# Four modulated residual blocks on one core: the first V and `conv0` in fp32, the first pair of samples blurred alone

## The reference

```
def _layer(x, style, w, b, mw, mb, typ):
    s = style @ mw.T + mb
    weight = SCALE * w * s[:, None, :, None]
    demod = lax.rsqrt(jnp.sum(weight * weight, axis=(2, 3)) + EPS)
    weight = weight * demod[:, :, None, None]
    # 'same': conv_same(x, weight) + b
    # 'upsample': conv_transpose by 2 + b, then blur with 2 * [1, 3, 3, 1] / 8
    # 'downsample': blur with [1, 3, 3, 1] / 8, then conv with stride 2, + b
...
for i, typ in enumerate(('same', 'upsample', 'same', 'downsample')):
    out = _layer(out, style, weights[i], biases[i], mod_w[i], mod_b[i], typ)
...
x = x + block(x)      # four times, each with its own weights
```

## Time and profile before

| | |
|---|---|
| median of 3 runs | 1302.7 us (1302.08 to 1303.91) |
| profiled execution, device time | 1303.89 us |
| its span (first to last instruction) | 1302.0 us |
| mean granted TensorE clock | 0.998 of 2.4 GHz |
| busy: PE, DVE, ACT, POOL | 99%, 85%, 71%, 28% |
| instructions | 20375 |

### The profile page before, as it was taken

One profiled execution on the slowest core, in us unless ns is written; L12 is line 12 of the kernel. 1 busy time (PEld: TensorE's weight loads), 2 busy tenths in 40 slices (PEclk: granted clock), 3 DMA queues, 4 the chain that ended last, 5 costly groups with the idle time before them and its releaser, 6 DMA issues.

```text
span 1302.0 us, 20375 instructions
## 1 busy us (share of the span) xinstructions
PE 1291.3 (99%) x6553; PEld 1076.5 (83%) x6553; DVE 1101.5 (85%) x1795; ACT 922.4 (71%) x1773; POOL 359.1 (28%) x640
## 2 busy tenths in 40 slices
PE   8999999999999999999999999999999999999998
PEld 6888888888888888888888888888888888888887
DVE  7999888998898889878889798988878878888885
ACT  6767576676675766766767667667677787787784
POOL 5142311141313212115222222122422252322311
PEclk9999999999999999999999999999999999999999
DMA  9354465545564455655446554556554276565543
GB/s 327 103 168 119 144 179 165 164 116 164 174 174 144 123 155 166 182 151 168 130 152 177 153 164 121 154 172 174 161 158 128 77 159 188 163 189 156 165 126 96
DMA packets 95369, 203.39 MB, mean 156 GB/s; under 512 B 10720, under 2 KB 12256, under 8 KB 95264
## 3 DMA queue, kind: packets, MB, share of 16 engines
q1 hardware_dynamic: 95040, 201.91, 54.0%
q10 hardware_dynamic: 224, 0.18, 0.0%
HBM read 72.39 MB, written 67.24 MB: 107 GB/s over the span
## 4 chain that ended last, share of the span: by engine, by line
PE 98%; DVE 1%; ACT 0%; issue 0%; POOL 0%; POOLq 0%; DVEq 0%; ACTq 0%
PE ps L462 96%; PE ps L586 1%; PE ps L398 1%; DVE scr L945 0%; ACT gh L815 0%; ACT vf L771 0%; PE ps L420 0%; DVE scr L955 0%; DVE scr L954 0%; DVE xl L1036 0%; DVE w2l L1245 0%; DVE w3q L1163 0%; ACT xh L733 0%; POOL scr L1416 0%; POOL scr L1415 0%
## 5 line engine op out<-in xcount | busy, mean ns | idle before, releaser
L462 PE MATMUL ps<-zh,gh 128*128 128x512 f32 (+1 forms) x1028 | 407.0, 396 | 0.2 <-ACT gh L815 0.2
L462 PE MATMUL ps<-zl,gh 128*128 128x512 f32 (+1 forms) x1028 | 405.5, 394 | 0.0
L747 ACT ACTIVATE zh<-ps,t_bx 128x512 fp32r<-128x512 f32 x256 | 175.3, 685 | 285.4 <-PE ps L462 284.4
L462 PE MATMUL ps<-zh,gl 128*128 128x512 f32 (+1 forms) x1028 | 282.2, 395 | 0.0
L787 ACT ACTIVATE kp<-ps,t_T1s 64x256 f32<-64x256 f32 x508 | 210.6, 463 | 66.3 <-PE ps L462 61.4
L1051 DVE SCALAR_TENSOR_TENSOR X<-ps,t_D,X 128x512 f32<-128x512 f32 x255 | 190.1, 745 | 61.1 <-PE ps L462 34.6
L462 PEld LDWEIGHTS ps<-zh,gh 128*128 128x128 f32 x1028 | 193.9, 189 | 46.9 <-DVE zl L1042 1.3
L462 PEld LDWEIGHTS ps<-zl,gh 128*128 128x128 f32 x1028 | 194.1, 189 | 45.0
L462 PEld LDWEIGHTS ps<-zh,gl 128*128 128x128 f32 x1028 | 194.0, 189 | 45.1
L1042 DVE SCALAR_TENSOR_TENSOR zl<-ps,t_bx,zh 128x512 fp32r<-128x512 f32 x256 | 190.7, 745 | 42.9 <-ACT zh L747 40.2
L1377 POOL TENSOR_TENSOR w3h<-w3q,w3h 64x256 fp32r<-64x256 f32 x63 | 69.1, 1097 | 548.5 <-ACT w3h L761 535.0
(11 more groups left out here) (226 smaller groups left out, 1494.5 us busy)
## 6 DMA issues: line engine op xcount, KB each, us to landing
out_x<-X SPq DMA_DIRECT2D x255, 256.5 KB, 5.2
X<-out_x SPq DMA_DIRECT2D x96, 513.0 KB, 7.1
gh<-gh SPq DMA_DIRECT2D x127, 240.0 KB, 3.0
gl<-gl SPq DMA_DIRECT2D x127, 240.0 KB, 3.7
X<-x_in SPq DMA_DIRECT2D x32, 513.0 KB, 7.2
pk<-taps_in SPq DMA_DIRECT2D x3, 512.0 KB, 12.3
pk<-pack_in SPq DMA_DIRECT2D x3, 352.0 KB, 12.5
pk<-sets_in SPq DMA_DIRECT2D x4, 256.0 KB, 8.4
```

The costliest lines, as they stand in the source:

```text
L462: return pe.matmul(out_ap, a, b, start=first, stop=last, skip_group_check=True)
L747: act.activation(zh[n % 2][:, ZPAD:ZPAD + M], ps[:, ZP + n % 2, :], IDENT, bias=tab["bx"][:, k, b:b + 1]).then_inc(s["zhi"], 1)
```

## The change

- V of quad 0 is four fp32 products of the unsplit `w2f` and `w3q` instead of nine fp32r ones; its splits (`w3h`, `w3l` of quad 0) are gone.
- `conv0` of samples 0, 1 and 2 (`WHOLE = 3`) is two fp32 products each, of `X` itself and a copy of the weights scaled by `S0` (`w0s`, made on ScalarE in place of `xhi`); their `xhi` and `xlo` are gone. `conv0(1)` comes before V of quad 1, `conv0(2)` right behind `convg(0)`.
- 14 idle products become 4 products of `w2h`; 6 earlier ones become 5.
- Quad 0 is evicted pair by pair: VectorE and ScalarE first evict samples 0 and 2 (they share one half of the columns of `kp`), whose blur runs at once (`fir0`), then samples 1 and 3; ScalarE takes two of VectorE's four evictions.
- VectorE's `w2l` comes first, `w2dl` and part of `w2d` move from GpSimd to VectorE. ScalarE's `ghi_first(0)` moves ahead of `vfull(1)`, `xhi(2)`, `w3hi(2)`; `w0hi` behind `w3hi(1)`.
- GpSimd waits for `w3qa` before it goes on; the tap sums come before `w1l` and `w1d`; the w3 product of quad 1 waits for V; `w3lo(1)` waits for `bx0`; the w3 product of quad 2 and `w0l` wait for `zlo` 1.

```diff
 def conv0(n):
...
+    if n < WHOLE:
+        p, use = pair_of(n)
+        pe.wait_ge(s_in[p], 16 * use)
+        xn = X[:, where(n)[3], :]
+        for d in range(2):
+            m = add(o, w0s[:, n % 2, 2 * d:2 * d + 2, :], xn[:, d:d + M], first=(d == 0), last=(d == 1))
+        m.then_inc(s["conv0"], 1)
+        return
...
 def v_products(q):
...
+    if q == 0:
+        pe.wait_ge(s["w2f"], 16)
+        pe.wait_ge(s["w3qa"], 1)
+        add(a[:, 0], w2f[:, 0, left, :], w3q[:, 0], first=True)
+        add(a[:, 1], w2f[:, 0, right, :], w3q[:, 0])
+        pe.wait_ge(s["w3q"], 1)
+        add(a[:, 1], w2f[0:C, 0, left, :], w3q[0:C, 1], last=True)
+        add(b, w2f[0:C, 0, right, :], w3q[0:C, 1], first=True, last=True).then_inc(s["V"], 1)
+        return
...
 conv0(0)
-conv0_high(1)
-idle_products(4)
+conv0(1)
 v_products(1)
-idle_products(14)
+for _ in range(4):
+    add(ps[:, OP + 1, 0:256], w2h[:, 0, 0:2, :], w2h[:, 0, :, :], first=True, last=True)
 pe.wait_ge(s["z0"], 1)
 for n in range(NN):
...
     if n == 0:
-        conv0_low(1)
         convg(0)
+        conv0(2)
         k_products(1)
-    elif n + 1 < NN:
+    elif 2 <= n and n + 1 < NN:
         conv0(n + 1)
...
 # ScalarE
 def xhi(n):
...
+    if n < WHOLE:
+        act.wait_ge(s["w0f"], 16)
+        if n >= 2:
+            act.wait_ge(s["conv0"], n - 1)
+        act.activation(w0s[:, n % 2], w0f[:, 0], ACT.Copy, scale=tab["S0"][:, 0, b:b + 1]).then_inc(s["xhi"], 1)
+        return
...
 act.wait_ge(s["t1s"], 1)
-for j in range(QS):
-    ins = evict(0, j, 0)
-ins.then_inc(s["kev"], 1)
+evict(0, 0, 0)
+evict(0, 2, 0).then_inc(s["kev0"], 1)
+evict(0, 1, 0)
+evict(0, 3, 0)
+act.wait_ge(s["kevd"], 1)
+evict(0, 1, 1)
+evict(0, 3, 1).then_inc(s["kev"], 1)
 zhi(0)
+act.wait_ge(s["z0"], 1)
+ghi_first(0)
+xhi(2)
+glo_copy(0)
 vfull(1)
...
 # VectorE
 dve.wait_ge(s["c_small"], 16)
+dve.wait_ge(s["w2hi"], 1)
+dve.wait_ge(s["w2f"], 16)
+dve.tensor_tensor(w2l[:, 0], w2f[:, 0], w2h[:, 0].bitcast(F32), ALU.subtract).then_inc(s["w2l"], 1)
...
-xlo(0)
 dve.wait_ge(s["t1s"], 1)
 dve.wait_ge(s["K"], 1)
-for j in range(QS):
-    ins = evict_first(j)
-ins.then_inc(s["kevd"], 1)
-dve.wait_ge(s["kev"], 1)
+step(evict_first(0))
+evict_first(2).then_inc(s["kevd"], 1)
+dve.wait_ge(s["kev0"], 1)
 dve.wait_ge(s["kz"], 1)
 dve.wait_ge(s["kevd"], 1)
-fir_first()
-xlo(1)
+settle()
+fir_first(slice(0, 1), "fir0")
 zlo(0)
 glo_first(0)
+dve.wait_ge(s["kev"], 1)
+fir_first(slice(1, 2), "fir")
 vlo(1)
...
 # GpSimd
-pool.wait_ge(s["K"], 1)
+pool.wait_ge(s["bx0"], 1)
 w3lo(1)
+pool.wait_ge(s["zlo"], 1)
 w3s(2)
+pool.wait_ge(s["w0hi"], 1)
+sig(pool.tensor_tensor(w0l[:, 0], w0f[:, 0], w0h[:, 0].bitcast(F32), ALU.subtract), "w0l")
```

More of the change, by code:

```diff
@@ L37 @@
 FIRST = 32
+WHOLE = 3
 NPART = 3
@@ L109, in build @@
         w0l = sb("w0l", [128, NW, 4, C], F32R)
+        w0s = sb("w0s", [128, 2, 4, C])
         w2h = sb("w2h", [128, NW, 4, C], F32R)
@@ L457, in _ @@
             first_style(0, EP).then_inc(s["Sp"], 1)
-            idle_products(6)
+            idle_products(5)
             def add(out_ap, a, b, first=False, last=False):
@@ L464, in conv0 @@
             def conv0(n):
-                conv0_high(n)
-                conv0_low(n)
-            def conv0_high(n):
                 k, o = where(n)[1], ps[:, ZP + n % 2, :]
-                ah, al, h = w0h[:, k % NW], w0l[:, k % NW], xh[n % 3]
+                ah, al, h, l = w0h[:, k % NW], w0l[:, k % NW], xh[n % 3], xl[n % 3]
                 pe.wait_ge(s["xhi"], n + 1)
@@ L480, in conv0_high @@
                     add(o, al[:, 2 * d:2 * d + 2, :], h[:, d:d + M])
[L482 to L485, removed]
+                pe.wait_ge(s["xlo"], n + 1 - WHOLE)
                 for d in range(2):
@@ L529, in v_products @@
                 left, right = slice(0, 2), slice(2, 4)
-                pe.wait_ge(s["w2hi"], k + 1)
[L531 to L535, removed]
+                if q == 0:
[7 more added lines that the diff above has]
+                    return
+                pe.wait_ge(s["w2hi"], k + 1)
+                pe.wait_ge(s["kev"], q)
+                pe.wait_ge(s["w3h"], q)
                 if q == 1:
@@ L752, in xb @@
                 st, k, b, sl = where(n)
-                act.wait_ge(s["xlo"], n + 1)
+                act.wait_ge(s["xlo"], n + 1 - WHOLE)
                 act.wait_ge(s["tabs"], NBLK)
@@ L859, in _ @@
             xhi(0)
+            xhi(1)
             act.wait_ge(s["vfa"], 1)
@@ L865, in _ @@
             w3hi(1)
-            xhi(1)
+            w0hi(0)
             act.wait_ge(s["K"], 1)
             act.wait_ge(s["t1s"], 1)
-            for j in range(QS):
-                ins = evict(0, j, 0)
-            ins.then_inc(s["kev"], 1)
+            evict(0, 0, 0)
[5 more added lines that the diff above has]
+            evict(0, 3, 1).then_inc(s["kev"], 1)
             zhi(0)
+            act.wait_ge(s["z0"], 1)
+            ghi_first(0)
+            xhi(2)
+            glo_copy(0)
             vfull(1)
             vhi(1)
[L875 to L878, removed]
             zhi(1)
-            glo_copy(0)
             ghi_first(1)
@@ L883, in _ @@
             xhi(3)
+            w3hi(2)
             glo_copy(1)
@@ L1106, in _, with fir_first @@
             whole, both = slice(0, 128), slice(0, 2)
[L1108 to L1112, removed]
+            def fir_first(i, name):
+                fir_even(whole, i)
+                step(dve.tensor_copy(gf[:, 0:NT:NT - 1, i, :], kp[:, 1:8:6, i, :]))
+                fir_odd(whole, i).then_inc(s[name], 1)
             def glo(q):
@@ L1253, in _ @@
             dve.tensor_tensor(T0["E1"], sall[:, 2, :], sall[:, 1, :], ALU.mult).then_inc(s["sall"], 1)
+            dve.tensor_tensor(w2d[0:C, 0, 3], w2f[0:C, 0, 2], w2h[0:C, 0, 2].bitcast(F32), ALU.subtract)
+            for h in range(2):
+                ins = dve.tensor_tensor(w2dl[h * C:(h + 1) * C, 0], w2f[0:C, 0, 0:2], w2h[0:C, 0, 0:2].bitcast(F32), ALU.subtract)
+            ins.then_inc(s["wl"], 1)
             dve.wait_ge(s["sall"], 1)
@@ L1338, in _ @@
         def _(pool):
-            counts, open_ = {"w3q": 1, "w3l": 1}, {}
+            counts, open_ = {"w3q": 1}, {}
             def sig(ins, name="chp", by=1):
@@ L1365, in w3s @@
                     pool.wait_ge(s["w3rest"], 16)
-                pool.wait_ge(s["w3l"], q)
+                if q == 1:
+                    pool.wait_ge(s["V"], 1)
+                else:
+                    pool.wait_ge(s["w3l"], q - 1)
                 if QS * q >= FIRST and k == 0:
@@ L1373, in w3lo @@
             def w3lo(q):
-                pool.wait_ge(s["w3h"], q + 1)
+                pool.wait_ge(s["w3h"], q)
                 fence()
@@ L1396, in _ @@
             sig(pool.tensor_copy(w2d[0:C, 0, 0:K], w2f[0:C, 0, 0:K]))
-            sig(pool.tensor_copy(w2d[C:128, 0], w2f[0:C, 0]))
+            sig(pool.tensor_copy(w2d[C:128, 0], w2f[0:C, 0]), "w2c")
+            fence()
+            pool.wait_ge(s["w3qa"], 1)
+            pool.wait_ge(s["wsq"], 1)
+            link(pool.tensor_tensor(wsum[:, 1:NLAY], wsq[:, 1:NLAY, 0, :], wsq[:, 1:NLAY, 1, :], ALU.add))
+            sig(pool.tensor_tensor(wsum[:, 1:NLAY], wsum[:, 1:NLAY], wsq[:, 1:NLAY, 2, :], ALU.add), "ws0")
+            fence()
             pool.wait_ge(s["w1ha"], 1)
             pool.wait_ge(s["w1t"], 16)
-            fence()
             hi, own = w1h[:, 0].bitcast(F32), w1d[:, 0].bitcast(F32)
@@ L1413, in _ @@
             fence()
[L1414 to L1417, removed]
             w3s(1)
-            pool.wait_ge(s["w0hi"], 1)
-            sig(pool.tensor_tensor(w0l[:, 0], w0f[:, 0], w0h[:, 0].bitcast(F32), ALU.subtract), "w0l")
-            fence()
             sig(pool.memset(kp[:, NONE], 0.0), "kz")
```

37 lines of the change are left out of this document (4 added, 33 removed), and 6 rows, old and new, of the table s.

## The result

| | before | after |
|---|---|---|
| median | 1303.54 us (1302.08 to 1305.38, 20 runs) | 1305.25 us (1302.75 to 1307.15, 20 runs) |
| profiled execution, its span | 1303.89, 1302.0 | 1305.98, 1304.2 |

The ratio of after to before is 1.0015, 95% interval 1.0009 to 1.0021: slower, by less than 0.2%. A repetition in another group of runs gave 1.0022 (1.0013 to 1.0032). The forecast was 1300.8.

The account below looks back on a forecast made before the run. TensorE's unbroken queue, busy 99% of the span, was taken to bound the kernel. The queue's move of -2.75 and the clock's -0.3 gave -3.05 on the profiled 1303.89: 1300.8 us, range 1298.6 to 1302.9.

Parts of the forecast that it names:

- To V of quad 0: Start of the kernel: VectorE reads V at 11.1 us against 11.69, -0.6; T1s at 16.4, -0.4.
- To the first blur: From T1s to convg(0): first pair's blur ends at 21.0, convg(0) at 22.3 instead of 26.31 us, -4.0.
- To sample 4: From convg(0) to xlo(4): second quad's blur at 34.8 instead of 37.53; tied to VectorE, the queue moves by -2.75 us.
- Clock, -0.3: At the start: denser TensorE work may raise the clock before V ends, gaining up to 0.5 us; 0.3 taken.
- Two signs of being wrong: At the start: the forecast is wrong if V is read after 11.7 us or the clock is low after 17.5.
- Behind it the order and the work of both kernels are the same, and TensorE never waited: Behind xlo(4), to the end: same order and work, no TensorE waits, so the queue stays moved by -2.75 us.
- third sign of being wrong: Behind the start: the forecast is wrong if TensorE waits anywhere after sample 4.
- The median: Whole kernel: before's profiled run lies 1.2 us above median 1302.7, so the sum is -1.9 against the median.
- Rival 2: Clock falls in the pause before V(2) or convg(0), costing at most 1.7, about 1.3 us: 1302.1; chance 0.15.
- Rival 1: At the start, GpSimd's jobs miss the blurs: second quad's blur -4.1 us, 1299.5; chance 0.35.
- Rival 3: At the start, the clock does not rise under fp32 products: blur at 38.8, +1.3 us, 1305.2; chance 0.07.

Follow-up runs that it names:

- a_again: After unchanged, run and traced again: 1306.84 us, with before at 1304.38 in the same group.
- a_fill: After with 12 filler products within the convolution ahead of the late pause: 1303.22 us, ratio 0.9988 to before.
- b_fill: Before with SyncE's stores spread evenly behind the tap copies and 28 instead of 14 filler products ahead of convg(0): 1302.07 us, ratio 0.9981 to before.
- a_hold: After with GpSimd's w3 product of quad 2 and w0l released by vl of quad 1 instead of zlo 1: 1307.29 us, one profiled run.
- a_clear: After with no store in SyncE's queue between the loads and quad 53's tap copies: 1301.63 us, ratio 0.9996 to before.
- a_together: After with the second pair's blur straight behind the first's, ahead of zlo(0) and glo_first(0): 1306.91 us, one profiled run.
- a_swap: After with SyncE issuing the loads of samples 216 to 223 and later ahead of the stores of finished samples: 1306.96 us.
- a_vsplit: After with V of quad 0 back to nine split products, GpSimd's tap sums behind the splits: 1308.85 us, one profiled run.
- a_late: After with 27 instead of 4 filler products ahead of convg(0): 1302.73 us, ratio 0.9985 to before.

## Why the prediction was wrong

- **To V of quad 0**: VectorE's Newton steps took 0.19 as forecast, V ran from 7.55 (7.3) for 4.05 us (3.5), and was read at 11.71, not 11.1: before had 11.69. The -0.6 was nothing. The term that was too small is the eight fp32 records at 1.2 GHz: 0.5 us each, not 0.44. `T1s` was done at 16.57 (16.4; 16.80 before), and not through V: the demodulation's products of the tap sums, moved ahead on GpSimd, let VectorE go on at 12.64 instead of 12.86. So a gain of 0.2 where 0.4 was forecast, for another reason.
- **To the first blur**: first add at 18.14, held 0.50 by `w3lo(1)`, first blur over at 21.26 (21.0) and `convg(0)` at 22.68 (22.3). Right.
- **To sample 4**: blur of pair two over at 26.63 (26.5), blur of quad 1 at 34.82 (34.8), queue moved by 2.75 (2.75). Right, and VectorE was the tie from there on; into that blur it had waited 0.29 us for ScalarE's evictions.
- **Clock, -0.3**: in the profiled run it rose at 18.6, after before's 16.7, so nothing. Two signs of being wrong, V read after 11.7 and the clock low after 17.5, came with it and cost nothing that shows. But the rise is chance with a larger price than I gave it: in a_again it rose at 9.1, V took 3.07 instead of 4.05 us and the lead was 3.70.
- **"Behind it the order and the work of both kernels are the same, and TensorE never waited"**: this step failed. The order was the same; the slack was not. Rows 3 list only waits that happened. The sum has no term for a wait behind sample 4; such a wait was its third sign of being wrong, and it came. SyncE's copies of quad 53 land between 1089.9 and 1092.0 in before, after and every version that left eight stores and the loads ahead of them, bar a_fill, whatever the lead was (0 to 3.7 us). A lead is turned into a pause there, and the pause brings a low stretch: +4.5.
- **The median**: I took before's profiled run as 1.2 us above its median, because it alone had paid 1.7 us for the low stretch. Over 20 runs the median is 1303.54, only 0.35 below it. b_fill shows 1.5 for the stretch. Part of the rest of the lead goes in the landing of the last store; why is not settled.
- **Rivals**: none had this. Rival 2 had a low stretch behind a pause at 1.7 us at most, but in the wrong place: the pause before V of quad 2 came (1.32 us) without one. Rival 1 priced the missing collision at 1.35 us at the start; a_hold shows 0.2. "Slower" was sought at the start, where the profile could be read closely, not at the far end, where I had looked at a sum.

Sum, with what was measured: 1303.89 - 2.63 + 4.53 + 0.3 (the last store landed later) = 1306.1; the profiled run took 1305.98.

## What to carry to other kernels

A list of waits shows which waits happened, not how little slack the others had: before a gain at the start of a long in-order queue is counted at the end, look for the places where a semaphore from another queue comes just in time. Small copies that TensorE needs belong ahead of bulk stores that nobody waits for. Where TensorE pauses and is then granted the lower clock, try filler products first: with the same order of stores, one changed number gave here what the rewritten start gave.

## What the runs showed of the hardware

- **The same eight stores and four loads (4.1 MB) took longer in the kernel where they began earlier.** From the first store ahead of the copies to their landing passed 27.1 us in after (1063.43 to 1090.55) and 24.1 in before (1065.79 to 1089.87). The last three figures of these rows are the clock, the busy share of the DMA engines and GB/s, for after:

```profile
1071.00:1075.00 4.00, 4.00 (x18) 3.22 (x18) 3.15 (x7) 3.17 (x5) 0.73 (x2) 1.00 1.29 119
...
1079.00:1083.00 4.00, 4.00 (x19) 3.24 (x18) 2.81 (x3) 3.92 (x9) 0.14 (x1) 1.00 1.06 381
```

  In the first stretch the first four stores are under way: 119 GB/s with every engine busy; in the second the loads, 381. Why the stores take longer in some runs than in others stays open. The Trainium skill (DMA: Bandwidth & Descriptors, "Queues, rings and completion order") has the copies of one issuing engine share rings on the same 16 DMA engines, each taken in ring order. By that rule a small copy stands behind the share of every copy issued ahead of it; the traces agree, 9.9 us behind stores (after) and 3.1 with the way clear (a_clear).
- **The clock and the pauses.** It was granted 0.50 for 3.4 us in or behind pauses of 2.09 (before), 2.49 (a_together), 2.85 (after) and 3.45 us (a_swap), for 6.8 us in and behind one of 4.24 (a_vsplit, hence its lag of 4.11), and not behind 1.32 (after) or 1.6 us (a_late). In a_again it was also low from 12.6 to 16.0, without a pause over 0.7 us; TensorE had been busy for 2.72 of the 3.40 us ahead.
- **The clock rises under fp32 products**: at 18.6 in after, within `conv0(0)` and `conv0(1)`, at 9.1 in a_again, within V. Rival 3 is out.
- **VectorE beside GpSimd** was held as forecast, until GpSimd's instruction ended: the first add took 0.50 instead of 0.21 us (to 18.64; GpSimd's second `w3lo` subtraction ended at 18.56), the second 1.05 instead of 0.21 (to 23.55; GpSimd's w3 product ended at 23.48).
